# Zeros of two attention stages written by ScalarE and VectorE instead of by transfers, and another order in the first group of the retention

## The reference

```
# retention (L0_xattn): 16 heads of 16 features
q, k, v = einsum('bld,hde->bhle', ...)        # q of the normalized x, k and v of the context
q, k    = _xpos(q), _xpos(k)                  # x * cos + rotated(x) * sin
sim     = einsum('bhnd,bhsd->bhns', q, k) * decay_mask
ret     = einsum('bhns,bhsd->bhnd', sim, v);  ret = (ret - mean) / sqrt(var + eps)
x       = x + ret * silu(xn @ g_w.T + g_b) @ out_w.T + out_b

# one-key attention (L1_xattn): 16 query heads, one key and one value head of 16 features
att = softmax(einsum('bhsd,btd->bhst', qp, kp) / sqrt(D));  x = x + einsum('bhst,btd->bhsd', att, vp)
```

## Time and profile before

| | |
|---|---|
| median of 3 runs | 1681.52 us |
| the profiled execution's own time | 1681.53 us |
| its span | 1679.8 us |
| PE / DVE / ACT / POOL busy | 77% / 62% / 48% / 40% |
| granted TensorE clock, mean | 0.823 of full |
| retention in the span | about 185 to 465 us |
| one-key attention in the span | about 1136 to 1412 us |

### The profile page before, as it was taken

One profiled execution on the slowest core, in us unless ns is written; L12 is line 12 of the kernel. 1 busy time (PEld: TensorE's weight loads), 2 busy tenths in 40 slices (PEclk: granted clock), 3 DMA queues, 4 the chain that ended last, 5 costly groups with the idle time before them and its releaser, 6 DMA issues. The chain is left out here.

```text
span 1679.8 us, 33514 instructions
## 1 busy us (share of the span) xinstructions
PE 1291.2 (77%) x12367; PEld 978.1 (58%) x12367; DVE 1043.9 (62%) x2051; ACT 803.4 (48%) x1528; POOL 674.5 (40%) x611
## 2 busy tenths in 40 slices
PE   5888567787864439999999738873788885699997
PEld 2555345666653338888888637632465653356664
DVE  5988447767665365555655474663788762576654
ACT  4767235566542424344444322131467686466653
POOL 1222249888881114444444300060378786000000
PEclk9989778888866559999999955555889785799999
DMA  7655666544614512322232180008442420230340
GB/s 273 223 198 209 162 122 119 90 77 80 93 20 165 239 51 64 102 87 89 85 101 77 45 321 1 2 1 158 115 74 59 77 34 2 102 115 26 114 127 26
DMA packets 107593, 173.12 MB, mean 103 GB/s; under 512 B 14758, under 2 KB 71338, under 8 KB 106156
## 3 DMA queue, kind: packets, MB, share of 16 engines
q1 hardware_dynamic: 98412, 146.06, 32.7%
q0 software_dynamic: 8640, 24.65, 4.7%
q10 hardware_dynamic: 384, 0.26, 0.1%
HBM read 110.60 MB, written 52.30 MB: 97 GB/s over the span
## 5 line engine op out<-in xcount | busy, mean ns | idle before, releaser
L2778 POOL TENSOR_TENSOR q_pl<-q_ex,q_ph 128x512 f16<-128x512 f32 x128 | 147.0, 1160 | 43.7 <-ACT q_ph L2739 43.0
L1756 POOL TENSOR_TENSOR r_siml<-r_sim,r_simh 128x512 f16<-128x512 f32 x128 | 146.2, 1162 | 30.5 <-ACT r_simh L1673 30.5
L1087 POOL DMA_INDIRECT expert_results<-mt_yout,m_deliver x78 | 77.4, 992 | 161.7 <-ACT mt_yout L1175 149.7
L2594 DVE TENSOR_REDUCE q_mx<-q_pS 128x4 f32<-128x512 f32 x128 | 86.6, 685 | 65.7 <-PE q_pS L2522 65.2
L1673 ACT ACTIVATE r_simh<-r_sim 128x512 f16<-128x512 f32 x128 | 79.9, 628 | 92.4 <-DVE r_sim L1547 88.4
L1547 DVE TENSOR_TENSOR r_sim<-r_pS,r_causal 128x512 f32<-128x512 f32 x128 | 86.6, 682 | 58.5 <-PE r_pS L1461 56.2
L1120 PE MATMUL mt_pU<-mt_xh,m_w 128*128 128x256 f16 x624 | 116.2, 274 | 1.5 <-DVE mt_xl L1205 1.5
L1120 PE MATMUL mt_pV<-mt_xh,m_w 128*128 128x256 f16 x624 | 115.0, 273 | 0.0
L1131 PE MATMUL mt_pY<-m_w,mt_hh 128*128 x624 | 106.5, 272 | 6.7 <-DVE mt_hl L1219 6.7
L1169 ACT ACTIVATE mt_hh<-ahead 128x512 f16<-128x512 f32 x78 | 49.1, 630 | 126.9 <-DVE ahead L1214 123.8
L1079 POOL DMA_INDIRECT mt_xin<-token_rows,m_fetch x78 | 82.2, 1054 | 68.0 <-POOLq L778 44.6
(11 more groups left out here) (515 smaller groups left out, 3977.4 us busy)
## 6 DMA issues: line engine op xcount, KB each, us to landing
s_spread_share<-shares SPq DMA_DIRECT2D x32, 512.0 KB, 7.7
a_pf<-in_L_ffn_W SPq DMA_DIRECT2D x24, 512.0 KB, 6.3
m_w<-split_w SPq DMA_DIRECT2D x6, 2048.0 KB, 22.2
split_w<-a_ph SPq DMA_DIRECT2D x24, 256.0 KB, 3.8
split_w<-a_pl SPq DMA_DIRECT2D x24, 256.0 KB, 4.3
r_kstack<-k_bounce SPq DMA_DIRECT2D x48, 128.0 KB, 4.6
r_qstack<-q_bounce SPq DMA_DIRECT2D x48, 128.0 KB, 6.0
q_Q<-m_bounce SPq DMA_DIRECT2D x24, 256.0 KB, 6.7
```

What stands on the lines that cost most here:

```text
L1087: pool.indirect_dma_start(results[:, :], bass.IndirectOffsetOnAxis(ap=deliver[:, at:at + 1], axis=0), yout[n % 2][:, a, :], None).then_inc ...
L1756: pool.tensor_tensor(siml[n % RING][:, :], sim[n % SIMS][:, :], simh[n % RING][:, :], ALU.subtract)\
L2594: dve.tensor_reduce(mx[:, at:at + UNIT], pS[n % 2][:, :, :], AX, ALU.max).then_inc(s["taken"], 1)
L2778: pool.tensor_tensor(pl[n % RING][:, :], ex[n % 3][:, :], ph[n % RING][:, :], ALU.subtract)\
```

## The change

In the retention, all six clearing transfers go. ACT writes the whole tiles `kstack0`, `qstack0`, `kstack1`, `qstack1` by a copy from the zeros tile (`clear`, 128x2048 words of 32 bits each), the first ahead of its first step and the other three after the first group's `rows_high` and `high`. DVE writes `kstack2` and `qstack2` by `memset` behind the first `rows_low`. Since whole tiles are written, the wait on `cleared` moves from PE's first scores to SP's first loads into each buffer.

In the same stage the first group goes another way: its rows are turned into `pB` (`turning(g)`), so PE waits only for `xn` there, and the wait for `k_sin` moves to the gate's projection. ACT makes `rows_high` ahead of `high("k")`. The preparation of the bias rows moves on ACT from ahead of the first step to t = -33 and on DVE from t = -41 (ahead of the statistics' `combine`) to t = -32.

In the one-key attention, ACT writes `Q0` ahead of its first step and `Q1` after the first `v_high`, and DVE writes `Q2` (128x4096 words each). The three transfers go, and the wait moves to `load_q`.

The two writes of zeros come after `r_xl`, ahead of the statistics of group 1. The diff:

```diff
@@ retention @@
+        def turning(g):
+            return pB if g == 0 else pA
+        def whole(t):
+            return t[:, :, :, :].rearrange("p h b t -> p (h b t)").bitcast(f32)
...
                     sp.wait_ge(stored[n][g % 2], 64 * (g // 2 + 1))
-                    if m >= HALVES:
+                    if m < HALVES:
+                        sp.wait_ge(cleared[m], 2)
+                    else:
                         sp.wait_ge(s["scored"], (m - HALVES + 1) * UNITS // 2)
...
-                for i in range(HALVES):
-                    for n in "kq":
-                        rest = stack[n][i][ROWS:P, :, :, :].rearrange("p h b t -> p (h b t)").bitcast(f32)
-                        sp.dma_start(rest.rearrange("p (n d) -> p n d", d=D), repeat(A["zeros"][ROWS:P, :], 2 * NH * S // (2 * D)))\
-                          .then_inc(cleared[i], 16)
...
                 def turn_rows(g, dc):
                     if dc == 0:
                         pe.wait_ge(s["xn"], GB * (g + 1))
-                        pe.wait_ge(s["k_sin"], g + 1)
+                        if g > 0:
+                            pe.wait_ge(s["k_sin"], g + 1)
                     for b in range(GB):
-                        last = pe.transpose(pA[:, dc, tokens(b)], xn[:, b, dc * P:(dc + 1) * P], ident[:, :])
+                        last = pe.transpose(turning(g)[:, dc, tokens(b)], xn[:, b, dc * P:(dc + 1) * P], ident[:, :])
...
@@ score @@
                     if u % 8 == 0:
-                        if m < HALVES:
-                            pe.wait_ge(cleared[m], 32)
...
@@ step of dve @@
-                    if t == -41:
+                    if t == -26:
+                        for n in "kq":
+                            dve.memset(whole(stack[n][2]), 0.0).then_inc(cleared[2], 1)
+                    if t == -32:
                         dve.wait_ge(s["bias_high"], 2)
...
+                def clear(n, i):
+                    act.activation(whole(stack[n][i]).rearrange("p (n d) -> p n d", d=D),
+                                   repeat(A["zeros"], NH * S // D), ACT.Copy).then_inc(cleared[i], 1)
...
@@ step of act @@
+                    if t == -33:
+                        act.wait_ge(s["bias_in"], 32)
+                        act.wait_ge(s["made"], 1)
+                        act.activation(rows[0:1, :], bias[0:1, :], ACT.Copy, scale=SCALE).then_inc(s["bias_high"], 1)
+                        act.activation(bias16[ONES:ONES + 1, :], bias[ONES:ONES + 1, :], ACT.Copy, scale=SCALE)\
+                           .then_inc(s["bias_high"], 1)
                     g = due(t, -29)
-                    if g is not None:
+                    if g is not None and g > 0:
                         high("k", g)
                     g = due(t, -28)
                     if g is not None:
                         rows_high(g)
+                        if g == 0:
+                            high("k", g)
+                            for n, i in (("q", 0), ("k", 1), ("q", 1)):
+                                clear(n, i)
...
+                clear("k", 0)
                 each_step(step)
@@ one_key_attention @@
                     sp.wait_ge(q_stored[g % 2], 16 * (g // 2 + 1))
-                    if g >= KEPT:
+                    if g < KEPT:
+                        sp.wait_ge(cleared[g], 1)
+                    else:
                         sp.wait_ge(s["scores"], (g - KEPT + 1) * UNITS)
...
-                for i in range(KEPT):
-                    rest = Q[i][KEY_ROWS:P, :, :, :].rearrange("p c b t -> p (c b t)").bitcast(f32)
-                    sp.dma_start(rest.rearrange("p (n d) -> p n d", d=D), repeat(A["zeros"][KEY_ROWS:P, :], SLOTS))\
-                      .then_inc(cleared[i], 16)
...
@@ step of dve @@
+                    if (i, u) == (-2, 15):
+                        dve.memset(whole(Q[2]), 0.0).then_inc(cleared[2], 1)
...
+                def clear(i):
+                    act.activation(whole(Q[i]).rearrange("p (n d) -> p n d", d=D),
+                                   repeat(A["zeros"], SLOTS * GT // (2 * D)), ACT.Copy).then_inc(cleared[i], 1)
...
                         if u == 13:
                             v_high(g)
+                            if g == 0:
+                                clear(1)
...
+                clear(0)
                 each_step(step)
```

More of the change, by code:

```diff
@@ L1535, in rows_low @@
                     dve.wait_ge(s["xh"], g + 1)
-                    dve.tensor_tensor(xl[:, :, :], pA[:, :, :], xh[:, :, :], ALU.subtract).then_inc(s["xl"], 1)
+                    dve.tensor_tensor(xl[:, :, :], turning(g)[:, :, :], xh[:, :, :], ALU.subtract).then_inc(s["xl"], 1)
                 def v_low(g):
@@ L1648, in rows_high @@
                         act.wait_ge(s["gate_projected"], DC * g)
-                    act.activation(xh[:, :, :], pA[:, :, :], ACT.Copy).then_inc(s["xh"], 1)
+                    act.activation(xh[:, :, :], turning(g)[:, :, :], ACT.Copy).then_inc(s["xh"], 1)
                 def high(n, g):
@@ L1725, in _ @@
                 nc.scalar.preload_act_table(ACT.Silu)
-                act.wait_ge(s["bias_in"], 32)
-                act.wait_ge(s["made"], 1)
-                act.activation(rows[0:1, :], bias[0:1, :], ACT.Copy, scale=SCALE).then_inc(s["bias_high"], 1)
-                act.activation(bias16[ONES:ONES + 1, :], bias[ONES:ONES + 1, :], ACT.Copy, scale=SCALE)\
-                   .then_inc(s["bias_high"], 1)
+                clear("k", 0)
                 each_step(step)
@@ L2376, in one_key_attention, with whole @@
         out = c.sb("out", [P, 2, NH, HD])
+        def whole(t):
+            return t[:, :, :, :].rearrange("p c b t -> p (c b t)").bitcast(f32)
         def keys(b):
@@ L2514, in measure @@
                     if u == 0:
-                        if g < KEPT:
-                            pe.wait_ge(cleared[g], 16)
                         pe.wait_ge(q_loaded[g % KEPT], 48 * (g // KEPT + 1))
```

## The result

The changed kernel takes **1668.33 us** (median, 1667.57 to 1669.15) against 1681.84 for the kernel before in the same set: ratio 0.9927, 95% interval 0.9915 to 0.9939. The forecast was 1663.3 us, with its own range of 1660 to 1667 inside a wider one of 1658 to 1669. The kernel is faster, by 13.5 us where 18.2 were forecast; both stops went, and the retention gave less than its term. The profiled execution took 1669.15 us (span 1667.4).

The account below looks back on a forecast made before the run. No engine was taken to bound the whole; PE, the busiest, idled 23%, and its idle time ahead of first scores mattered. 1681.5 - 8.8 (retention) - 9.4 (one-key attention) = 1663.3 us, range 1660 to 1667 inside 1658 to 1669.

Parts of the forecast that it names:

- both stops: PE's waits behind queued zero transfers: 3.92 us for group 1's context in the retention, 15.75 us ahead of one-key first scores.
- the one-key term: One-key attention: without the queue of zeros the first scores start at 1166.9 instead of 1176.28, a gain of 9.4 us.
- the retention's term: Retention: group 1's rows are turned at 216.4 instead of 225.22, and the whole 8.8 us is kept.
- the 3.5 us at `r_xl`: Retention, group 0: DVE starts the low part of the turned rows at 198.1 instead of 201.56, so q comes 3.5 us earlier.
- the rival's row of 1.19 us: Rival, retention: DVE's zeros and POOL block each other, as in a 1.19 us DVE operation; 1663.5 to 1664.9, inside the range.
- 7.3 were forecast: Retention: PE starts k of group 1 at 208.5 instead of 215.81, 7.3 us earlier.
- `memset` price of 1.76: Retention: each DVE `memset` of 2048 words takes 1.76 us; the upper bound was 2.45, another estimate 2.13.
- nothing on the path: Retention: DVE's two `memset`s end before q of group 0 comes at 203.9, so they delay PE by nothing.
- PE's pace behind the stop: Retention: without the 3.92 us stop PE keeps its gate pace through k, v, k up to group 1's turning, 1.5 us more.
- Only one stop goes: Rival: either the one-key store is slow by itself (1670.9 us) or later retention groups take back 8.8 us (1672.1); chance 0.10.
- Slower: Rival: ACT's zeros, read from one repeated 256-word row, cost f times a plain copy; 1684 us at f = 3.5; chance 0.03.
- 16.4 - 5.8 f: Retention's gain if ACT's zero writes cost f times a plain copy; with the one-key attention nothing is left at f = 3.2.

Follow-up runs that it names:

- bias_early: The changed kernel with DVE's low bias row written at t = -35, ahead of its first reading of k, not t = -32; 1657.34 us, ratio 0.9906.
- ret_all: The kernel before with only the retention's half of the change (zeros and first group's order), one-key attention as before; 1669.02 us, ratio 0.9979.
- ret_delay: `ret_all` with five waited-for `memset`s on POOL at the end of the stage `lie`; 1667.19 us, ratio 0.9971.
- after_again: The changed kernel run once more, unaltered, on chip 1; 1658.34 us, ratio 0.9920.
- warm_ret: `bias_early` with 16, 12 and 12 unread filler matmuls in three of PE's waits in the retention; 1653.36 us, ratio 0.9878.
- onekey_only: The kernel before with only the one-key attention's half of the change, retention as before; 1663.10 us, ratio 0.9939.
- before_delay: The kernel before with five waited-for `memset`s on POOL at the end of the stage `lie`; 1672.70 us, ratio 1.0005.
- warm_one: `bias_early` with 24 unread filler matmuls on PE ahead of the one-key attention's first scores, none in the retention; 1652.87 us, ratio 0.9877.

## Why the prediction came out 5 us low

**Right.** Both stops of PE were the transfers' doing, and both went. The store-to-load distance of the one-key attention came out at 3.48 us where 2.96 were taken from group 1, the scores 9.34 behind the load where 9.06 were taken. The prices of ACT's writes were right within 0.02 us, 1.91 and 3.62, and ACT had the room for them. The zeros of DVE stretched nothing on POOL (2.14 us beside them, 2.12 before).

**Right in part by luck: the one-key term**, 9.4 us forecast, 9.1 measured. The working had q of group 0 done where it was before. It was done 2.0 us earlier, 16.3 us behind the start, because PE projected it at the upper level of the clock (0.38 us a product, before 0.63 for the most part); with the old code three executions had it at 16.3 and three at 17.9 to 18.2, so the change has no part in that. With the two distances 0.8 us too short, the first scores came 10.6 us earlier and not 9.4; by the stage's end 1.5 of it was gone, which the working had put at nothing. Two errors nearly cancelled.

**Wrong: the retention's term**, 8.8 us forecast, 6.3 measured. Two steps of it failed.

The first is the 3.5 us at `r_xl`. The working laid the moved bias row into DVE's list with the 0.68 us of its old place and didn't ask what POOL does at the new one. It reads two SBUF operands, like the rival's row of 1.19 us, and met POOL's addition; the rival spoke of such contention and put it only to the `memset`s. The Trainium skill, "SBUF — State Buffer", section on who interferes with whom, says both: DVE with two SBUF inputs contends with a GpSimd instruction that reads SBUF, with one or none, outside the two-port modes, it doesn't. The trace agrees with each half: 1.59 against 0.68 us for the bias row, and the same 2.14 us for the `memset` beside POOL's low part and the one beside an idle POOL. With 0.9 for this and 0.3 for the later end of k, 2.3 us were left of 3.5. Of the 1.2 missing 0.8 reached k of group 1, 6.5 where 7.3 were forecast. `bias_early` takes the cause away. The `memset` price of 1.76 was too low as well, by 0.38 us each; of that only 0.15 us reached PE here, 0.3 in `ret_all`, `ret_delay` and `after_again`, but PE's stop of 1.60 us in `warm_ret` shows that "nothing on the path" held for want of a faster PE.

The second is larger: "PE's pace behind the stop", 1.5 us, and with it the assumption that the lead at group 1's turning is the lead at the end of the stage. At the turning the lead was 8.2 us, near the forecast; at the first `r_sim` 7.3, at the last 6.5. The turning in the profile of before was itself a poor measure. With the same retention and its stop in place it stands 37.8 us behind the stage's start in `onekey_only` and 37.7 in `before_delay`, not 39.9. Windows of the kernel before and of `onekey_only`, 30 to 52 us behind that start:

```profile
215.40:237.40 22.00, 14.05 (x65) 8.14 (x66) 8.81 (x18) 4.92 (x6) 7.75 (x5) 0.69 0.53 97
```

```profile
216.50:238.50 22.00, 13.92 (x75) 8.13 (x76) 9.15 (x18) 5.04 (x7) 8.38 (x6) 0.77 0.65 120
```

The same code got 65 matmuls at a granted 0.69 in the one and 75 at 0.77 in the other. On chip 4, `ret_all` against `onekey_only`, the lead is 6.3 us at k of group 1, 6.3 at its turning and 6.1 at the last `r_sim`; on chip 7, `ret_delay` against `before_delay`, 6.2, 6.2 and 6.2. Between k and the turning, where the working booked 1.5 us, nothing is gained. So the 1.5 us were the clock's level in one profiled execution, booked as the stop's. That a later group keeps a lead only if PE's clock allows it is what `bias_early` (1.3 us of lead gone by the 33rd `r_sim`) and `warm_ret` (level with `warm_one` at the turning, 3.4 ahead of it at the end) point to from both sides.

**Not foreseen: unchanged stages.** The forecast had all other stages as long as before. In the profile they came out 3.0 us longer (0.7, 2.0, 0.2 and 0.1). The experiments put this outside the change: the first stage varied from 184.1 to 186.5 us among kernels that have it alike, and `moe_swiglu` came at 435.4 to 435.6 or 437.2 to 437.4 on all three chips. 2.5 for the retention, 0.3 for the one-key attention and 3.0 for the rest make 5.8 us: 1663.3 + 5.8 = 1669.1, the profiled execution; the median is 0.8 lower.

**The rivals.** "Only one stop goes" fell: both went. "Slower" by ACT's form of reading fell: 1.91 us is the plain pace. (By its own numbers its first gain is 16.1 - 5.8 f, not 16.4 - 5.8 f; the 3.2 stays.) No rival held that a stage without a changed line takes another time from one execution to the next, 2.0 us in `moe_swiglu` and 5.9 in the old one-key attention. That should have been one, at 2 to 5 us either way.

## What to carry to other kernels

An instruction's time belongs to its place: when one with two SBUF operands is moved, look at what POOL or DVE does beside it at the new place, and take the duration beside it. Booking a lead at the head of a pipelined stage as a gain at its end needs PE at the same clock level in both; read the granted clock over the stretch before taking a pace from it, and take a pace from more than one execution. Time a `memset` from the end of the instruction before it, not by its row alone. Removing transfers paid only together with the order that used the freed time: neither half of the retention's change gained anything in the timed runs (0.9996 and 1.0025), both together 0.9979.

## What the runs showed of the hardware

- The same instructions took 273.2 to 279.1 us as the old one-key attention, 435.4 to 437.4 as `moe_swiglu`, and 328.9 to 332.4 as the retention of `bias_early`. In `moe_swiglu` the difference is the step of the clock, which fell into a given 5 us or behind them, at a busy PE. A pause of 2.1 us between two stages cost the whole nothing in `ret_delay` (0.9971, 0.9979 without it).
- 40 filler matmuls in PE's stops took 3.4 to 6.9 us from a stage of 329 to 332 us, though they kept PE busy for 9.1 us: they ran where PE waited. In the two windows the granted clock was 1.00 with them, 0.90 and 0.77 or 0.94 and 0.81 without. The Trainium skill, "TensorE: Matmul & The Clock Gate", section on HAM oscillation, describes a kernel whose waits between groups of matmuls pull the clock down, and a new order of the loops against it; the trace agrees, and shows that useless matmuls keep it up as well.
- A `memset` of 2048 32-bit words a partition took DVE 2.14 us and one of 4096 words 4.27, of which its row in the profile shows 1.76 and 3.47.
- A one-row `scalar_tensor_tensor` of 0.68 us took 1.59 beside a POOL addition, which grew from 2.48 to 2.93; both engines lose.
